# One factor of the expert marks on GpSimd, VectorE's last round of self-attention in another order, and the border of blocks behind the first gathers

## The reference, cut to what matters

```
x = x + cross_attention(layernorm(x), ctx)     # 16 heads, 257 keys
x = x + self_attention(layernorm(x))           # tanh scores over earlier positions, tanh output
x = x + experts(layernorm(x))

def experts(x):                                # 8 experts, the best 2 of each token
    gate = softmax(x @ Wg.T); val, idx = top_k(gate, 2); val = val / (sum(val) + 1e-9)
    for e in range(8):
        a, b = split(x @ W1[e].T + b1[e]);  g = a * sigmoid(b)
        out += (g @ Wo.T + bo) * comb[..., e]
```

## Time and profile before

| | |
|---|---|
| median of three runs | 633.14 us |
| profiled execution, own time | 629.26 us |
| its span (first to last instruction) | 627.5 us |
| mean granted TensorE clock | 0.989 of full speed |
| TensorE busy | 596.4 us (95%) |
| VectorE, ScalarE, GpSimd busy | 459.9, 339.7, 331.5 us |

### The profile page before, as it was taken

One profiled execution on the slowest core, in us unless ns is written; L12 is line 12 of the kernel. 1 busy time (PEld: TensorE's weight loads), 2 busy tenths in 40 slices (PEclk: granted clock), 3 DMA queues, 4 the chain that ended last, 5 costly groups with the idle time before them and its releaser, 6 DMA issues. The chain is left out here.

```text
span 627.5 us, 21706 instructions
## 1 busy us (share of the span) xinstructions
PE 596.4 (95%) x8364; PEld 484.3 (77%) x8364; DVE 459.9 (73%) x1073; ACT 339.7 (54%) x743; POOL 331.5 (53%) x482
## 2 busy tenths in 40 slices
PE   9999999999999999999999999896999999998786
PEld 3788878888788887888886788773578888884574
DVE  3687877888678786777776755989799977773453
ACT  3677868788688776778774346541222233330121
POOL 3357858777677885788872322221433333306561
PEclk9999999999999999999999999996999999999999
DMA  8624643766355836973300992119533433435774
GB/s 242 154 68 108 175 167 110 237 180 206 115 172 162 215 127 202 231 209 123 123 3 22 413 412 99 35 49 373 183 127 128 141 136 126 129 116 154 207 210 117
DMA packets 65204, 102.10 MB, mean 163 GB/s; under 512 B 15408, under 2 KB 42096, under 8 KB 64080
## 3 DMA queue, kind: packets, MB, share of 16 engines
q1 hardware_dynamic: 59808, 86.42, 42.7%
q0 software_dynamic: 4432, 13.50, 7.8%
q10 hardware_dynamic: 864, 0.79, 0.5%
HBM read 69.42 MB, written 31.26 MB: 160 GB/s over the span
## 5 line engine op out<-in xcount | busy, mean ns | idle before, releaser
L537 DVE TENSOR_SCALAR Pm<-scores 128x514 f32<-128x514 f32 x128 | 88.1, 688 | 57.0 <-PE scores L750 56.9
L653 ACT ACTIVATE Pm<-Pm,nm 128x257 f32<-128x257 f32 x256 | 115.8, 505 | 2.5 <-DVE nm L542 2.5
L542 DVE TENSOR_REDUCE nm<-Pm 128x2 f32<-128x514 f32 x128 | 87.5, 684 | 2.2
L1634 POOL DMA_INDIRECT Xg<-y_d,inv x39 | 37.1, 951 | 87.1 <-PE scores L1821 69.9
L648 ACT ACTIVATE PT<-bank 128x512 f32<-128x512 f32 x64 | 38.2, 598 | 74.5 <-PE bank L761 74.5
L731 PE MATMUL bank<-hA,wH 128*128 128x258 f32 x256 | 75.3, 305 | 0.1
L738 PE MATMUL bank<-wH,hA 128*128 128x256 f32 x256 | 74.3, 301 | 0.5 <-DVE PT L549 0.5
L761 PE MATMUL bank<-cst,Pm 128*128 128x128 f32 x512 | 69.9, 279 | 0.0
L731 PE MATMUL bank<-hA,wL 128*128 128x258 f32 x256 | 69.1, 280 | 0.0
L738 PE MATMUL bank<-wL,hA 128*128 128x256 f32 x256 | 68.9, 280 | 0.0
L1836 PE MATMUL bank<-W,xh 128*128 x208 | 66.7, 402 | 1.0 <-DVE xl L1744 1.0
(11 more groups left out here) (262 smaller groups left out, 1442.2 us busy)
## 6 DMA issues: line engine op xcount, KB each, us to landing
w_d<-whl SPq DMA_DIRECT2D x64, 256.0 KB, 3.4
W<-w_d SPq DMA_DIRECT2D x8, 2048.0 KB, 15.4
g_d<-gg SPq DMA_DIRECT2D x39, 256.0 KB
wst<-in_W1T SPq DMA_DIRECT2D x32, 256.0 KB, 3.6
cx<-in_ctxT SPq DMA_DIRECT2D x31, 258.0 KB, 2.9
cx<-in_ctxT SPq DMA_DIRECT2D x62, 129.0 KB, 3.5
bb<-in_b SPq DMA_DIRECT2D x8, 512.0 KB, 12.6
xb<-in_x SPq DMA_DIRECT2D x4, 512.0 KB, 5.5
```

Source lines behind the costliest of these rows:

```text
L537: v.tensor_scalar(Pm[:, i % 2, 2 * p:2 * p + 2, :], S4[:, 2 * p:2 * p + 2, 0:NK], -CLAMP, CLAMP, ALU.max, ALU.min).then_inc(s_cl, 1)
L542: v.tensor_reduce(nm[:, i % 2, 2 * p:2 * p + 2], Pm[:, i % 2, 2 * p:2 * p + 2, :], AX.X, ALU.max, negate=True).then_inc(s_nm, 1)
L653: a.activation(Pm[:, i % 2, g, :], Pm[:, i % 2, g, :], ACT.Exp, bias=nm[:, i % 2, g:g + 1]).then_inc(s_ex, 1)
L1634: g.indirect_dma_start(out=Xg[:, i % 3, :], out_offset=None, in_=y_d, in_offset=bass.IndirectOffsetOnAxis(ap=inv[:, i:i + 1], axis=0)).the ...
```

## The change

Bv is written by GpSimd for chunks 0 to 2 and for the second half of chunk 3; VectorE keeps A16 and Bv's first half of chunk 3. In round 5 VectorE does the last `final_norm` ahead of `chosen(2)`, ScalarE copies both halves of gh, TensorE transposes yn ahead of `rank(2)`, and `marks(2)` follows `chosen(3)`. The routing of the last chunk and `inv` move into block 2. GpSimd issues its first three gathers in block 2, so that the border lies behind them; the tile table `ew` and the gate weights stay in block 3. The diff's pieces stand here in this order: the helpers of the marks, VectorE's round 5 and its end of block 2, GpSimd's and TensorE's end of block 2, GpSimd's start of block 3. `gather` is the body of the old loop.

```diff
+        def places(e, c, k):
+
+            return e.tensor_tensor(Bv[:, 4 * k:4 * k + 4, :].rearrange("p j (e t) -> p j e t", t=16),
+                                   oht[:, k, :, :].unsqueeze(3).broadcast_to([128, 4, E, 16]),
+                                   T16[:, 4 * k:4 * k + 4, :].unsqueeze(2).broadcast_to([128, 4, E, 16]), ALU.mult)
         def marks(v, c):
 
             if c:
                 v.wait_ge(u_iv, c)
             for k in range(2):
-                v.tensor_tensor(Bv[:, 4 * k:4 * k + 4, :].rearrange("p j (e t) -> p j e t", t=16),
-                                oht[:, k, :, :].unsqueeze(3).broadcast_to([128, 4, E, 16]),
-                                T16[:, 4 * k:4 * k + 4, :].unsqueeze(2).broadcast_to([128, 4, E, 16]), ALU.mult)
+                if c == 3 and k == 0:
+                    v.wait_ge(u_t16, 4)
+                    places(v, c, k)
                 v.tensor_tensor(A16[:, 4 * k:4 * k + 4, :], i16[:, :].unsqueeze(1).broadcast_to([128, 4, 128]),
                                 rf[:, 0, k, :].unsqueeze(2).broadcast_to([128, 4, 128]), ALU.is_equal).then_inc(u_ab, 1)
...
                     if k == 5:
                         best(2)
-                        chosen(2)
                     if 0 <= k - 2 < 4:
                         final_norm(k - 2)
+                    if k == 5:
+                        chosen(2)
...
-                    if k == 5:
-                        gate_in()
-                    if 0 <= k - 3:
+                    if 0 <= k - 3 < 2:
                         marks(v, k - 3)
...
+                marks(v, 2)
+                positions(v, link, 3, bank("r", 3))
+                marks(v, 3)
+                v.wait_ge(u_c2, 16)
...
+                v.wait_ge(r_i, 1)
+                v.tensor_copy(inv[:, :], bank("inv")[:, 0:40]).then_inc(r_iv, 1)
...
+                def placed(c):
+
+                    g.wait_ge(u_t16, c + 1)
+                    if c:
+                        g.wait_ge(u_iv, c)
+                    for k in range(c == 3, 2):
+                        places(g, c, k).then_inc(u_bv, 1)
...
                         biased(k - 1)
+                    if k >= 3:
+                        placed(k - 3)
+                placed(3)
+                g.wait_ge(r_iv, 1)
+                g.wait_ge(f_yd, 64)
+                for i in range(3):
+                    gather(g, i)
...
+                rank(t, 3, take("r", 3))
                 slots(t, 2)
+                busy(2)
+                slots(t, 3)
+                b = take("inv")
+                t.wait_ge(r_sel, 2)
+                t.matmul(b[:, 0:40], iT[:, :], sel[:, :], start=True, stop=True).then_inc(r_i, 1)
+                busy(2)
 
...
-                g.wait_ge(r_iv, 1)
-                g.wait_ge(f_yd, 64)
-                for i in range(NS):
-                    if i >= 3:
-                        g.wait_ge(e_t, i - 2)
-                    g.indirect_dma_start(out=Xg[:, i % 3, :], out_offset=None, in_=y_d,
-                                         in_offset=bass.IndirectOffsetOnAxis(ap=inv[:, i:i + 1], axis=0)
-                                         ).then_inc(e_x[i % 3], 16)
+                for i in range(3, NS):
+                    gather(g, i)
```

More of the change, by code:

```diff
@@ L882, in build @@
         bb = put("bb", [128, E, 1024])
+        area(155, 158)
+        Xg = put("Xg", [128, 3, C])
+        area(25.875, 26.03125)
+        inv = put("inv", [128, 40], I32)
+        area(26.21875, 26.3125)
+        tj = put("tj", [128, 3, E])
         u_y = sem("u_y")
@@ L919, in build @@
         u_iv = sem("u_iv")
+        u_t16 = sem("u_t16")
+        u_bv = sem("u_bv")
+        e_x = [sem(f"e_x{i}") for i in range(3)]
+        e_t = sem("e_t")
+        r_sel = sem("r_sel")
+        r_i = sem("r_i")
+        r_iv = sem("r_iv")
         f_st = sem("f_st")
@@ L961, in build @@
             if k == 5:
-                uses += [(("idle",), u_o, 8), (("r", 2), u_rk, 3)]
+                uses += [(("idle",), u_o, 8)]
             if 0 <= k - 2 < 4:
                 uses += [(("t3", k - 2, h), f_hi, 2 * (k - 2) + h + 1) for h in range(2)]
+            if k == 5:
+                uses += [(("r", 2), u_rk, 3)]
             if 0 <= c < 4:
@@ L968, in build @@
                 uses += [(("g", k - 2), f_gl, k - 1)]
+            if k == 5:
+                uses += [(("r", 3), u_rk, 4), (("inv",), r_iv, 1)]
         place = {u[0]: n for n, u in enumerate(uses)}
@@ L982, in build, with gather @@
         pI = B[7]
+        cnt = [0]
+        def gather(g, i):
+            if i >= 3:
+                g.wait_ge(e_t, i - 2)
+            g.indirect_dma_start(out=Xg[:, i % 3, :], out_offset=None, in_=y_d,
+                                 in_offset=bass.IndirectOffsetOnAxis(ap=inv[:, i:i + 1], axis=0)
+                                 ).then_inc(e_x[i % 3], 16)
         def rank(t, c, b):
@@ L1003, in slots @@
                 t.wait_ge(u_ab, 2 * c + k + 1)
+                if c < 3 or k:
+                    t.wait_ge(u_bv, 2 * c + k + 1 - (c == 3))
                 for j in range(4 * k, 4 * k + 4):
@@ L1012, in positions @@
             v.wait_ge(u_r2, c + 1)
+            if c:
+                v.wait_ge(u_bv, 2 * c)
             v.tensor_tensor(pr[:, :, :, :], oh[:, :, k, :],
@@ L1236, in _ @@
                         busy(1)
-                        rank(t, 2, take("r", 2))
                     if 0 <= k - 2 < 4:
                         lifted(k - 2)
+                    if k == 5:
+                        rank(t, 2, take("r", 2))
                     if 0 <= c < 4:
@@ L1523, in gate_in @@
                 def gate_in(c):
-                    for h in range(2 - (c == 3)):
+                    for h in range(2):
                         a.wait_ge(f_t, 2 * c + h + 1)
@@ L1551, in _ @@
                         outs(k - 1)
-        area(155, 167)
-        Xg = put("Xg", [128, 3, C])
+        area(158, 167)
         xh = put("xh", [128, 2, 2, 128], F32R)
@@ L1564, in build @@
         ew = put("ew", [1, 2, 40], I32)
-        area(25.875, 26.3125)
-        inv = put("inv", [128, 40], I32)
+        area(26.03125, 26.3125)
         pi = put("pi", [128, 2, NTILE], I32)
-        tj = put("tj", [128, 3, E])
         area(26.3125, 26.8125)
@@ L1577, in build @@
         fo = put("fo", [128, 4, C])
-        r_c = sem("r_c")
-        r_sel = sem("r_sel")
         r_pi = sem("r_pi")
-        r_i = sem("r_i")
-        r_iv = sem("r_iv")
-        r_ew = sem("r_ew")
         r_b3 = sem("r_b3")
-        e_x = [sem(f"e_x{i}") for i in range(3)]
-        e_t = sem("e_t")
         e_hi = sem("e_hi")
@@ L1679, in _ @@
             def _(v):
-                cnt = [0]
                 def link(ins):
                     cnt[0] += 1
-                    ins.then_inc(r_c, 1)
-                    v.wait_ge(r_c, cnt[0])
+                    ins.then_inc(u_ch, 1)
+                    v.wait_ge(u_ch, cnt[0])
                 v.tensor_tensor(gs[:, 1, :], g8[:, :, 1], g8[:, :, 0], ALU.subtract).then_inc(f_gs, 1)
@@ L1804, in busy @@
                                  skip_group_check=True)
-                busy(3)
-                slots(t, 3)
-                t.wait_ge(r_sel, 2)
-                t.matmul(B[1][:, 0:40], iT[:, :], sel[:, :], start=True, stop=True).then_inc(r_i, 1)
-                busy(2)
                 t.wait_ge(r_iv, 1)
                 busy(3)
-                t.wait_ge(r_ew, 2)
+                t.wait_ge(r_sel, 4)
                 t.wait_ge(w_r, 128)
```

51 lines of the change are left out of this document (18 added, 33 removed).

## The result

The changed kernel took **638.33 us** (median of 10 runs, 636.4 to 640.64), the kernel before beside it 631.64 us (628.8 to 635.35, 10 runs). The ratio is **1.0098, 95% interval 1.0072 to 1.0123**. The forecast of 644 us was against the 633.14 known then. 633.14 x 1.0098 is 639.3, between rival 1 (638) and the forecast, and nearer to rival 1. By the ratio the change costs 6.2 us (the two medians alone lie 6.7 apart), just under the 6.3 us of 1%; its interval reaches past 1%. So "slower by over 1%" is neither borne out nor refuted by this measurement.

What follows compares the result with a forecast made beforehand. TensorE is busy 596.4 of 627.5 us, so little can be won except where it waits. Border and what follows +9.6, clock +1.0, `inv` +0.6 make +11.2 us on the median 633.14: 644 us, range 635 to 649.

Steps and rivals of the forecast that it cites:

- rival 1: At the border behind the gathers, GpSimd's DRAIN waits for the issues only: about +5 us, 638; chance 0.20.
- slower by over 1%: Whole kernel: the changed one takes over 6.3 us longer; chance 0.67.
- Part 1: Second border: GpSimd's DRAIN behind three gathers holds all engines until 9.5 us behind `inv`.
- Both bounds: DRAIN's end at the border: 4.1 us behind `inv` if only issues count, 10.0 if as at the program's end.
- Part 2: Release to first expert product: table and gate weights no longer overlap the gathers, 5.6 us; `inv` to product +9.6 us.
- Part 3: TensorE around the release: the clock falls and three keep-busy products take 4.8 us, +1.0 us, bounds 0 and 4.
- Part 4: Ahead of `inv`: GpSimd's Bv products block VectorE, which also sheds work; `inv` +0.6 us, bounds -2.3 and +3.
- the second half of Ab: Round 3: a GpSimd Bv product gets between Ab's halves and delays the second by some 1.0 us.
- the wait for the scales: Last round on VectorE: 0.4 us of waiting, since `final_norm(3)` now stands ahead of `chosen(2)`.
- The wait for the last gate result: Last routing on VectorE: 0.4 us given back by waiting for that result.
- Rival 2: Border passed with gathers still queued, 0.3 us instead of 9.5; without blocking of VectorE -1.9, 631; chance 0.06.
- Rival 3: GpSimd's Bv products are twice as dear: +2.4 us more, 647, also with the long DRAIN; chance 0.08.

Runs made afterwards that it cites:

- e8: Changed kernel, but GpSimd waits until its three gathers' rows have landed before its DRAIN at the border; one run, no ratio, first product 13.55 us behind `inv`.
- e2: Changed kernel with one gather instead of three ahead of GpSimd's signal at the border; one run, no ratio, first product 9.36 us behind `inv`.
- e4: Changed kernel with Bv of chunks 0 and 1 back on VectorE; GpSimd keeps chunk 2 and one product of chunk 3; 638.25 us, ratio 1.0104.
- e11: Changed kernel with all Bv products back on VectorE and `marks(2)` again ahead of `chosen(3)`, gathers still ahead of the border; 634.12 us, ratio 1.0101.
- e3: Changed kernel with the tile table, gate weights and ScalarE's two exponentials also moved ahead of the border; 638.70 us, ratio 1.0113.
- repeat: The changed kernel itself measured once more in a later session, nothing altered; 634.31 us, ratio 1.0109 to the kernel before.
- e1: Changed kernel with all gathers issued behind the border again, `inv` still ahead of it; 635.99 us, ratio 1.0055.
- e9: Changed kernel with all gathers behind the border and without TensorE's two keep-busy products behind the product of `inv`; 629.30 us, ratio 1.0029.
- e10: Kernel before with only VectorE's new order, ScalarE's copy of gh and GpSimd's Bv products of chunks 2 and 3; 628.90 us, ratio 1.0019.

## Why the prediction was right, and where its sizes were off

The profiled shift of the first product was forecast at +11.2 and measured at +7.76 us.

- **Part 1, the border behind the gathers: the mechanism right, the term mis-sized.** GpSimd's DRAIN is what everyone waits for. Its release was put 9.5 us behind `inv`, measured 6.0: -3.5. Both bounds held (4.1, 10.0). I took the row at the program's end at nearly its full 6.95 us behind the last issue, though the chain shows that gather landing 4.0 behind its issue. At the border the DRAIN ends with the landing (e8), 2.9 behind the issue. So the step that was mis-sized is the 6.95 us from the last issue to the DRAIN's end: it measured 2.9. The row to trust was the landing, not the length. The Trainium skill (PSUM — Partial Sum Buffer, Engine vs sequencer instructions) says that a drain waits until the engine is fully idle. Read as "until the issuing is over" that gives 4.1, which was rival 1; the trace puts the end 2.0 us behind the end of the last issue, so here transfers in flight count as well.
- **Rival 1** had the mechanism wrong and the size 1.9 us short. That its 638 is nearer to the result (639.3) than the forecast's 644 is luck and does not bear it out; e2 and e8 speak against it. The time alone could not tell the two apart, since 639.3 lies in both spans (638 to 649 and 635 to 641).
- **Part 2, release to product: right to 0.3 us.** 5.6 forecast. In e2, where the keep-busy products ran at the full clock (2.81 us), 448.10 to 453.67 is 5.57, in the changed kernel 449.75 to 455.37 is 5.62. Counted from the DRAIN's end, as the forecast did, 0.3 us come on top of both. `ew` ends 2.65 us behind the DRAIN's end (2.7 forecast).
- **Part 3, the clock:** it fell as forecast, the three products took 4.28 us (4.8 expected), but VectorE's chain ends at 454.34, as late as TensorE's, so it cost next to nothing instead of +1.0. It was a near thing: in e4, e8 and e11 the same three products ran at half clock throughout (5.46 us), TensorE became the longer path, and 5.62 became 6.85 to 7.00, the +1.0 and a little more. e3 shows what the two paths hide from each other: the table off the path earns nothing.
- **Part 4, `inv`:** +0.6 forecast, +1.35 measured. Right: the price of GpSimd's product (1.3; median 1.222), the second half of Ab +0.83 (1.0), TensorE's wait 2.89 (3.1), `chosen(3)` held back 0.7 (0.7), though in its cast and not in its comparisons, the wait for the scales 0.5 (0.4). In `marks(3)` it was VectorE's Bv and not A16 that met the GpSimd product, for 0.9 (1.15). The wait for the last gate result (0.4) did not come. Missed: TensorE's longer wait in round 3 was followed by a fall of the clock, so `third(3)` started 2.46 us later instead of 1.1. The last round and the routing made 1.1 of it good (0.5 expected). That the longer wait caused the fall is not shown: in e4 the wait was as short as before and the clock fell too.
- **Rival 2** needed the border to be passed with gathers queued; e2 shows even one gather holding it until 3.5 us behind `inv`. **Rival 3** needed 2.6 us per product and fell with 1.222.
- **The sum:** -3.5 (Part 1), -0.7 (Parts 2 and 3), +0.75 (Part 4) is -3.45, which takes +11.2 to +7.75. The ratios make it 6.2 (first) and 6.8 us (repeat) in time. The call "slower by over 1%" at 0.67 rested on the 9.5; with 6.0 the sum is +7.7, little over the 6.3 us of 1%. The first ratio, 1.0098, falls just short of that and the repeat, 1.0109, just over it, both with intervals on both sides: by this term the call was worth no more than an even chance.

## What to carry to other kernels

Before a border is moved behind a DMA that GpSimd issues itself, ask when that DMA lands, not when it has been issued: every engine then waits for the landing. Keep-busy work issued just ahead of a border is also something that the border waits for (e1 against e9). And work moved off one engine into the gaps of another is worth only what the next waiter sees: here seven products moved and nothing was gained, and moving them back (e11) brought `inv` forward by 1.8 us and left the ratio where it was.

## What was not expected of the hardware

- GpSimd's DRAIN behind indirect gathers: 5.93 us with three, 3.47 with one, 0.316 once they had landed. With none at the same border it took 1.15, nearly all of it the product still running.
- A GpSimd product of 128x512 f16, both factors broadcast: median 1.222 us, 1.05 at the least; VectorE's takes 0.69, but 1.57 where it met one.
- A cast of 8 values per partition took 0.88 instead of 0.17 us beside such a product; it has one input, not two. The Trainium skill (SBUF — State Buffer, Who interferes with whom) has one of the two engines block for the other's whole instruction when VectorE's runs in a two-port mode, which it says a cast can enter, and has a VectorE instruction with two SBUF inputs contend with a GpSimd one that reads SBUF. The trace agrees on T16, Ab and Bv, which end 0.1 to 0.6 us behind the GpSimd instruction that they met; whether the cast ran in such a mode, no run here shows.
- Whether the clock falls in round 3 is a near thing: e4, e10 and e11 have the same work there, and it fell in e4 (0.66 over 404 to 409) and not in e10 and e11 (1.00).
- One stage, the gathers of results, took 46.4 and 47.5 us in the first profiles of the two kernels and 42.1 in the later one of the changed kernel, from the same code; what differs there between the sessions was not looked for.
